# Attention stage of a graph kernel: index lists copied by ScalarE, the outer product paced by the carry difference, sums placed between the segment maxima

## What is computed

```python
def _L1_gnn_ref(feat, efeat, W_msg, b_msg, W_attn, b_attn, src, dst):
    w_m = (efeat @ W_msg + b_msg).reshape(E, in_f, -1)
    w_a = (efeat @ W_attn + b_attn).reshape(E, in_f, -1)
    h_src = feat[src][:, :, None]
    e1 = w_m * h_src
    e2 = w_a * h_src
    seg_max = jax.ops.segment_max(e2, dst, num_segments=N)
    ex = jnp.exp(e2 - seg_max[dst])
    denom = jax.ops.segment_sum(ex, dst, num_segments=N)
    attn = ex / denom[dst]
    ft = jax.ops.segment_sum(e1 * attn, dst, num_segments=N)
    return ft.sum(axis=1)
```

## Time and profile before

| | us |
|---|---|
| time, median of 3 runs | 9014.39 (9012.21 to 9017.54) |
| the profiled execution's own time | 9001.38 |
| its span | 8999.6 |
| VectorE busy in the span | 7362.0 |
| attention: first to last `rescaled` (391 steps) | 3746.8 |
| narrow pass and preparation ahead of attention | some 1340 |
| three narrow passes behind it, from some 5300 | some 3700 |

### The profile page before, as it was taken

One profiled execution on the slowest core, in us unless ns is written; L12 is line 12 of the kernel. 1 busy time (PEld: TensorE's weight loads), 2 busy tenths in 40 slices (PEclk: granted clock), 3 DMA queues, 4 the chain that ended last, 5 costly groups with the idle time before them and its releaser, 6 DMA issues.

```text
span 8999.6 us, 248471 instructions
## 1 busy us (share of the span) xinstructions
PE 7062.4 (78%) x98927; PEld 6651.3 (74%) x98927; DVE 7362.0 (82%) x14062; ACT 1515.0 (17%) x3469; POOL 5189.3 (58%) x4569
## 2 busy tenths in 40 slices
PE   6999957777777777777777529999689999599994
PEld 6988956666666666666666429999589999599994
DVE  7888849999999999999999867777577777477774
ACT  0000003333333333333333310000000000000000
POOL 3555556666666666666666555555545555455554
PEclk9999978888888888888888769999899999799997
DMA  2222214444444444444444321111111111111110
GB/s 88 83 80 81 82 28 117 129 131 130 129 132 130 131 129 132 128 133 128 133 128 133 121 65 45 47 44 48 26 47 44 48 44 43 30 44 48 44 47 21
DMA packets 794679, 758.24 MB, mean 84 GB/s; under 512 B 210209, under 2 KB 754785, under 8 KB 794561
## 3 DMA queue, kind: packets, MB, share of 16 engines
q1 hardware_dynamic: 649088, 668.17, 23.3%
q0 software_dynamic: 140528, 86.77, 6.0%
q10 hardware_dynamic: 5008, 2.59, 0.1%
HBM read 240.60 MB, written 519.73 MB: 84 GB/s over the span
## 4 chain that ended last, share of the span: by engine, by line
PE 36%; DVE 28%; issue 17%; POOL 3%; DVEq 1%; DMA 0%; ACT 0%; POOLq 0%; SPq 0%; ACTq 0%
PE ps L791 36%; DVE amax_room L1169 5%; DVE spare L1174 5%; DVE ps L905 4%; DVE wide_buf L905 4%; DVE flat L1200 3%; DVE stt L905 3%; DVE flat L905 2%; POOL got L466 2%; DVE spare L1182 1%; POOL wide_buf L466 1%; POOL flat L466 0%; POOL z_room L466 0%; DVEq L1257 0%; PE ps L772 0%
## 5 line engine op out<-in xcount | busy, mean ns | idle before, releaser
L466 POOL DMA_INDIRECT msg<-feat,cidx x1680 | 1728.7, 1029 | 1703.8 <-PE ps L791 1338.9
L791 PE MATMUL ps<-parts,wide_buf 128*128 128x112 bf16 x42336 | 2172.9, 213 | 366.6 <-DVE wide_buf L1059 270.3
L791 PEld LDWEIGHTS ps<-parts,wide_buf 128*128 128x128 bf16 x42336 | 2109.5, 98 | 419.2 <-issue 416.2
L466 POOL DMA_INDIRECT hsrc<-feat,aidx x1568 | 1704.6, 1087 | 1229.8 <-DMA aidx<-src_sorted 842.0
L791 PE MATMUL ps<-parts,flat 128*128 128x112 bf16 x42336 | 2167.0, 213 | 88.0 <-issue 75.8
L791 PEld LDWEIGHTS ps<-parts,flat 128*128 128x128 bf16 x42336 | 2099.4, 98 | 143.1 <-issue 131.8
L838 PE MATMUL ps<-wsb,zT 102*128 102x192 f32 (+1 forms) x9408 | 1981.2, 372 | 140.8 <-ACT zT L694 133.3
L838 PEld LDWEIGHTS ps<-wsb,zT 102*128 102x128 f32 x9408 | 1813.8, 232 | 364.7 <-ACT zT L694 351.3
L831 PE MATMUL ps<-idm,z_room 128*102 128x128 f32 x4704 | 825.4, 323 | 985.1 <-DVE wide_buf L905 872.3
L831 PEld LDWEIGHTS ps<-idm,z_room 128*102 128x102 f32 x4704 | 649.3, 155 | 1058.7 <-issue 645.4
L905 DVE TENSOR_TENSOR raw<-ps,amask 128x336 f32<-128x336 f32 (+1 forms) x672 | 534.5, 851 | 899.2 <-PE ps L791 470.1
(11 more groups left out here) (209 smaller groups left out, 4015.7 us busy)
## 6 DMA issues: line engine op xcount, KB each, us to landing
state_tab<-flat SPq DMA_DIRECT2D x784, 512.0 KB
raw<-quot_tab SPq DMA_DIRECT2D x224, 576.0 KB
run_tab<-run SPq DMA_DIRECT2D x224, 224.0 KB
top_tab<-spare SPq DMA_DIRECT2D x392, 128.0 KB
msg<-feat,cidx POOLq DMA_INDIRECT x1680
hsrc<-feat,aidx POOLq DMA_INDIRECT x1568
efs<-in_ef SPq DMA_DIRECT2D x392, 34.0 KB
msg<-in_x,cidx POOLq DMA_INDIRECT x560
```

What stands on the lines that cost most here:

```text
L466: return pool.indirect_dma_start(dest, None, table, rows_at(idx))
L791: last = nc.tensor.matmul(block[:, 0:QW].rearrange("p (q c) -> p q c", c=D), hot[s][:, m, t * P:(t + 1) * P], parts[:, m * Q:(m + 1) * Q, ...
```

## The change

Three parts, all inside attention:

1. `aidx` is no longer loaded by SyncE: the whole list `sidx` has been in SBUF since the first narrow pass, and ScalarE copies 4 columns of it (`indices`), between the two pieces of `turned`. While it works on group g it copies the list of group g+3, after the gathers of group g+1 have landed (`a_got`).
2. `outer` waits for `a_gap` (the carry difference of g-3 is done), and no longer for `a_d`. VectorE now computes `gap` behind the last `differences`, not ahead of it.
3. In VectorE's step the differences and sums stand between the segment maxima in another order, maxima 2 and 0 signal a semaphore of their own (`a_top_of`), which also releases `put_top`; the exponential of the gap has a wait and a semaphore of its own (`a_gap`, `a_egap`).

```diff
@@ SyncE
-                def next_idx(j, s):
-                    sp.wait_ge(a_got[s], j * (16 * G))
-                    sp.sem_inc(s_sp, 1)
-                    load_idx(j, s)
...
                 def put_top(j, s):
-                    sp.wait_ge(a_d[s], 2 * j + 2)
+                    sp.wait_ge(a_top_of[s], 2 * j + 2)
@@ GpSimd
                 def fetch(j, s, first):
-                    pool.wait_ge(a_idx[s], 16 * (j + 1))
+                    pool.wait_ge(a_idx[s], j + 1)
...
-                            pool.wait_ge(a_d[1 - s], 2 * (j - 1 + s))
+                            pool.wait_ge(a_gap[1 - s], j - 1 + s)
@@ ScalarE
+            def indices(j, s, first=False):
+                if not first:
+                    act.wait_ge(a_got[s], j * (16 * G))
+                nc.scalar.activation(aidx[:, s, :], sidx[:, bass.ds((2 * j + s) * G, G)], ACT.Copy).then_inc(a_idx[s], 1)
...
+            def gap_weights(j, s):
+                act.wait_ge(a_gap[s], j + 1)
+                nc.scalar.activation(egap, egap, ACT.Exp).then_inc(a_egap[s], 1)
...
-                turned_all(j, s)
+                turned(j, s, 0)
+                if ask:
+                    indices(j + 1 + s, b)
+                turned(j, s, 1)
                 weights(jb, b, 0)
                 masks(j, s, first)
                 weights(jb, b, 1)
+                gap_weights(jb, b)
@@ VectorE, step
                     running_sum(jb, b, 0)
                     need(m)
-                    m = segment_max(s, 2)
+                    segment_max(s, 2).then_inc(a_top_of[s], 1)
+                    differences(s, 3, 4)
                     running_sum(jb, b, 1)
-                    differences(s, 3, 4)
+                    dve.wait_ge(a_top_of[s], 2 * j + 1)
+                    m = mark(segment_max(s, 1))
+                    differences(s, 2, 3).then_inc(a_d[s], 1)
+                    running_sum(jb, b, 2)
+                    dve.wait_ge(a_top, 16 * (2 * j + s))
                     need(m)
-                    m = segment_max(s, 1)
-                    running_sum(jb, b, 2)
-                    need(m)
-                    differences(s, 2, 3).then_inc(a_d[s], 1)
-                    dve.wait_ge(a_top, 16 * (2 * j + s))
-                    m = segment_max(s, 0)
+                    segment_max(s, 0).then_inc(a_top_of[s], 1)
                     running_sum(jb, b, 3)
-                    need(m)
-                    gap(s)
+                    dve.wait_ge(a_top_of[s], 2 * j + 2)
                     differences(s, 0, 2).then_inc(a_d[s], 1)
+                    gap(s)
```

More of the change, by code:

```diff
@@ L291, in gnn_program @@
         a_mm = ring("a_mm")
+        a_top_of = ring("a_top_of")
         a_d = ring("a_d")
         a_exp = ring("a_exp")
+        a_egap = ring("a_egap")
         a_w = ring("a_w")
@@ L404, in attention_moves @@
                 put_top(0, 1)
-                next_idx(3, 0)
                 next_ef(2, 1)
-                with sp.Fori(1, AHALF - 3) as j:
-                    round_(j, True, True, True)
-                round_(AHALF - 3, True, False, True)
+                with sp.Fori(1, AHALF - 2) as j:
+                    round_(j, True)
                 for j in range(AHALF - 2, AHALF):
-                    round_(j, False, False, False)
+                    round_(j, False)
                 put_states(AHALF - 1, 1)
@@ L689, in _, with turned @@
             asked(st3[:], st2[:], ACT.Sqrt)
[L692 to L699, removed]
+            def turned(j, s, piece):
+                for i, k in enumerate(range(*TURNS[piece])):
+                    act.wait_ge(a_tr[s], j * G + piece * HG + i + 1)
+                    nc.scalar.activation(zT[0:CW, 3 * k:3 * k + 3, :],
+                                         ps[0:CW, s * G + k, 0:3 * P].rearrange("p (c q) -> p c q", q=P), ACT.Copy).then_inc(a_trs[s], 1)
+            def indices(j, s, first=False):
+                if not first:
+                    act.wait_ge(a_got[s], j * (16 * G))
+                nc.scalar.activation(aidx[:, s, :], sidx[:, bass.ds((2 * j + s) * G, G)], ACT.Copy).then_inc(a_idx[s], 1)
             def weights(j, s, piece):
@@ L718, in group @@
                 weights(jb, b, 1)
-            turned_all(0, 0)
+                gap_weights(jb, b)
+            for s in range(2):
+                indices(0, s, True)
+            indices(1, 0)
+            for piece in range(2):
+                turned(0, 0, piece)
             masks(0, 0, True)
+            indices(1, 1)
             group(0, 1, True)
-            with act.Fori(1, AHALF) as j:
+            with act.Fori(1, AHALF - 2) as j:
                 for s in range(2):
                     group(j, s)
-            for piece in range(2):
-                weights(AHALF - 1, 1, piece)
+            for j in range(AHALF - 2, AHALF):
+                for s in range(2):
+                    group(j, s, ask=2 * j + s + 3 < AG)
+            weights(AHALF - 1, 1, 0)
+            weights(AHALF - 1, 1, 1)
+            gap_weights(AHALF - 1, 1)
             asked(ab[:], ab[:], ACT.Exp)
@@ L1186, in weighted @@
                     lo, hi = TURNS[piece]
-                    dve.wait_ge(a_exp[s], j * NEXP + piece + 1)
+                    dve.wait_ge(a_exp[s], 2 * j + piece + 1)
                     return tt(ebuf[:, s, lo:hi, DD:2 * DD], msgs[s][:, lo:hi, :], ebuf[:, s, lo:hi, 0:DD], ALU.mult).then_inc(a_w[s], 1)
                 def rescaled(j, s):
-                    dve.wait_ge(a_exp[s], j * NEXP + 3)
+                    dve.wait_ge(a_egap[s], j + 1)
                     return mark(tt(stt[:], st[:, 1 - s, G - 1, 0:2 * DD].rearrange("p (t c) -> p t c", t=2),
@@ L1247, in attention @@
                     need(running_max(0, k))
+                segment_max(0, 2).then_inc(a_top_of[0], 1)
                 differences(0, 3, 4)
-                for k in range(G - 2, -1, -1):
-                    need(segment_max(0, k))
+                dve.wait_ge(a_top_of[0], 1)
                 differences(0, 2, 3).then_inc(a_d[0], 1)
+                need(mark(segment_max(0, 1)))
+                segment_max(0, 0).then_inc(a_top_of[0], 1)
+                dve.wait_ge(a_top_of[0], 2)
+                differences(0, 0, 2).then_inc(a_d[0], 1)
                 gap(0)
-                differences(0, 0, 2).then_inc(a_d[0], 1)
-                dve.wait_ge(a_d[0], 2)
                 step(0, 1, False, False)
```

26 lines of the change are left out of this document (6 added, 20 removed).

## The result

| | before | after |
|---|---|---|
| time, median of 4 runs, us | 9015.70 (9012.21 to 9017.54) | 8801.89 (8801.48 to 8813.62) |
| the profiled execution, its span | 9001.38, 8999.6 | 8813.62, 8811.8 |
| attention, first to last `rescaled` | 3746.76 | 3532.90 |
| `rescaled`, sum and mean | 492.0, 1255 ns | 277.6, 708 ns |

The ratio of the times is 0.9766, with a 95% interval of 0.975 to 0.9783. The forecast was 8797, 5 us under the median and inside the range. So attention is compared by its own windows from here on.

The account below looks back on a forecast made before the run. VectorE, busy 98.7% of attention, was taken as the bound, with a 9.55 us step. Freeing `rescaled` gives 225 us, less deductions 217, so 9014.4 − 217 = 8797 us; range 8780 to 8850, chance 0.80.

Parts of the forecast that it names:

- The held instruction: VectorE's `rescaled`, both inputs in SBUF, stands still while GpSimd's product reads SBUF: mean 1255 ns, minimum 681.
- The place of the product: GpSimd's product starts 0.08 us after the gap's end and finishes 0.34 ahead of `rescaled`, which falls to 0.68.
- The sum: Whole kernel: 225 us of `rescaled`'s excess less deductions, 217 taken off 9014.4, gives 8797 us.
- The start: First collisions in attention stay: a sum of 3.16 us and the next `rescaled`, about 2 us of the excess.
- GpSimd's round: GpSimd's product, wait and four gathers of 1.15 to 1.25 us take 8.4 to 8.8 us, under 9.0.
- The new order: VectorE's reordered differences and sums add no bare dependence: cost 0; one would cost 78 us.
- Who keeps the port: VectorE against GpSimd in SBUF: trace contradicts that the first issuer holds the port; otherwise gain 11 us smaller.
- (a): GpSimd's gathers slow beside VectorE's sums, product late: 8865 us at 9.2 a step, 8905 at 9.3; chance 0.08.
- (b): VectorE has one more bare wait, or part of one: 8835 to 8875 us; chance 0.06.
- (c): TensorE stays at 1.2 GHz and sets a step of 10.2 us: 9255 us, slower than before; chance 0.03.
- (d): ScalarE's index copy is late by its wait, product arrives at its old place: 9000 to 9020 us; chance 0.03.

Follow-up runs that it names:

- e4: Kernel before, with its outer product cut from the third group on to one edge of four, lists still by DMA: 8804.98 us, ratio 0.9763.
- e1: Kernel before, with only the index lists copied by ScalarE; old order and old pace kept: 8792.68 us, ratio 0.9755.
- e5: Changed kernel, with the product waiting for the first weighted product, the instruction after the gap: 8525.85 us, ratio 0.9807.
- e6: Changed kernel, with the product's wait for the gap removed: 9171.87 us, ratio 1.0551.
- e7: Changed kernel, with the first running maximum moved ahead of the first weighted product: 8466.43 us, ratio 0.9741.
- e2: Changed kernel, with the index lists loaded by SyncE's DMA again, new order and new pace kept: 9039.87 us, ratio 1.0029.
- e3: Changed kernel, with the product waiting for the last difference instead of the gap: 8789.98 us, ratio 0.9749.
- e10: Changed kernel, with the index copy at the head of ScalarE's group and the first running maximum ahead of the first weighted product: 8737.63 us, ratio 0.9691.

## Why the prediction was right, point by point

- **The held instruction** was read rightly. A shorter product frees it (e4), an earlier one too (e1), one 0.6 us later holds it by 0.12 (e5), and a product beside the gap holds the gap (e6). The 0.55 or 0.56 us between the product's end and that of a held `rescaled` stands in all of them, but for 6 steps of e4. The short steps of the kernel before are of 9.00 to 9.01 us in 16 cases and 8.92 in one, where the prediction has 8.9 to 9.0; this changes nothing in its sum.
- **The place of the product** came as predicted: 0.08 behind the gap's end (in every other step 0.17 to 0.19), `rescaled` at 0.69, the step 9.00 to 9.02.
- **The sum**: 217 us were forecast for attention, 213.9 measured. The excess left in `rescaled` is 392 × (0.708 − 0.680) = 11 us, where 8 were forecast: about 8 in the steps of the 13 late products (4 to 9 forecast), 1.2 in the start's `rescaled` of 1.91, and 2 in the ordinary ones, which take 0.685 where the sum had 0.680.
- **The start** was costed at about 2 us of `rescaled`'s excess beside a held sum. The held sum came back too, as 3.22 us, the 3.16 of the earlier trace rows.
- **GpSimd's round** held two errors that worked against each other. I took 1.15 to 1.25 us for a gather, and the mean is 1.06. I put the first gather 0.77 behind the product, and missed that ScalarE's copy stands behind a `zT` pair that waits for a slow pass of TensorE: of the waits of the first gather, 235 were for the copy, 259.2 us in all, 1.5 at most. The round came out at 8.09 us in the median where 8.4 to 8.8 were forecast, but at over 8.9 in 54 of 351 steps. At a step of 9.0 that was within the slack; at the 8.8 of e7, 196 of 351 products had to follow straight on a gather.
- **The new order** cost nothing, as forecast, but not by itself: e2 shows parts 2 and 3 alone 29 us slower than before. The prediction never asked what each part would bring alone. It worked the moved pace into the chain of the gain; e1 has the old pace and the whole gain.
- **Who keeps the port** was the step that failed. I took recorded starts for issue times and concluded that the trace went against the second half of the rule of the Trainium skill. From this e3 was expected to hold the gap, and the gap took its 0.47 us. It did not reach the sum, since with the changed pace the two hardly meet.
- **The rivals** did not come. (a) needed a round of 9.0, and the waits for the gap (285.7 us in 290 steps) show it was under that. (b) VectorE's only idle time in the steps is 0.12 us before one running maximum, 388 times and 48 us in all, as in the kernel before: no bare dependence was added. (c) The granted clock in attention is 0.85, from 0.83. (d) The copy was late in many steps, but by less than GpSimd's slack.

## What to carry to other kernels

A busy engine with one instruction whose mean is far above its minimum on the same shape is probably held, and the other engine's row that ends a fixed time ahead of the held one's end names the holder. Look then for what sets the holder's place, here a 2 KB DMA issued at the end of the other's step, and move that; a pace only helps once everything ahead of it is early. After such a gain the next one may need two edits at once: moving a list copy gave 0, moving a maximum 17 us, both 49 us of attention.

## What the runs showed of the hardware

- Two instructions that both read SBUF by VectorE and GpSimd exclude one another in both directions: 0.47 became 2.87 us for the gap (e6), and 2.07 became 2.23 for the product (e3). In 6 steps of e4 both were longer than bare at once, which stays unexplained.
- The difference of two recorded starts does not tell who holds the port: with the same 0.5 us between them, the gap was held in 125 steps of e6 and free in 67 of e3.
- GpSimd idles 1.4 to 2.2 us between two gathers where 0.30 is usual, 13 times in attention, in all 13 traces. It is tied to the count of gathers and not to time: in every trace it comes first ahead of the 114th gather of attention and then ahead of each 112th after it, whether a step takes 8.8 us or 10.6, and whoever brings the lists. What it is stays open; no run was aimed at it.
- The kernel before takes 9011 to 9019 us in two sets and 8693.73 in the other, which ran on another chip. Attention's step is the same there (8.80 in e7, 8.79 in e10); the time is gone from the stages around it (attention starts at 1258 to 1262 us in the second set and at 1365 to 1376 in the others). In the first 600 us of e7 TensorE got through 10425 matmuls, in those of e10 through 9442, at a granted clock of 0.97 in both, so TensorE's clock does not explain it; the cause is open.
